# Layer 3 of a four-layer graph network: projections copied in pairs from two PSUM banks, and the first two aggregations of a group issued ahead of the next projection

## The chip, the core and the metric

The kernel runs on one core of one Trainium2 chip. The metric is the device time of one execution in microseconds (us). The core has five engines that work side by side, each through its own list of instructions in order: TensorE (PE, matrix products), VectorE (DVE), ScalarE (ACT), GpSimd (POOL) and SyncE (SP, which here only issues transfers). They meet through semaphores: an instruction waits until a counter has reached a value. PSUM, into which TensorE writes its products, has eight banks of 128 x 512 f32.

## The reference, cut to what matters

64 graphs of 128 nodes with 256 features each pass through four layers. After each layer comes a residual sum and a layer norm. The last layer, which the change touches, is per graph:

```python
def _L3_gnn_ref(x, A_shape, w, a):
    y = x @ w
    s = y @ a
    A = s[..., :, None] + s[..., None, :]
    A = jnp.tanh(A / 8.0) * 8.0
    A = jnp.where(A >= 0, A, 0.1 * A)
    A = jnp.exp(A) * A_shape
    A = A / jnp.sum(A, axis=-1, keepdims=True)
    A = A * jnp.sum(A_shape, axis=-1, keepdims=True)
    return A @ x @ w
x = _layernorm(x + _L3_gnn_ref(x, adj, w, a))
```

## The kernel before, in words

The graphs are worked on in 16 groups (g) of four graphs (j = 0 to 3). Each layer is a software pipeline: every engine has a function `step(g, p, has)` that issues its work for one step, for groups at different stages. `has(0)` is the group g itself, `has(-1)` the one before. No planner sets the order: it is written out by hand in these functions, and each engine keeps to it. Only at the seams between two layers do the steps of both layers alternate, by strings such as `SEAMS_PE`.

In layer 3 the work of a group is this.

1. TensorE makes the node scores from the transposed features xT (`node_scores`, 24 products of one column, lines 87 to 89). VectorE splits them in two halves (`split_scores`, lines 1502 and 1504).
2. TensorE spreads the scores over a 128 x 512 tile (`spread_scores`, line 1514, 8 products). ScalarE takes the tanh in four operations (line 1982), VectorE the leaky step (line 2028), ScalarE the exponential (line 1989). GpSimd multiplies by the adjacency and gives U (line 2076, `attention`).
3. TensorE makes x @ w of each graph (`project(g, p, j)`, 6 products of 256 columns at lines 87 to 89), graphs 0 and 2 in one bank, graphs 1 and 3 in the next (`b_xw[j % 2]`). ScalarE copies each to SBUF (`copy_xw`, line 1974), and only then may its bank be written again.
4. TensorE multiplies U by that copy in f32 (`aggregate(g, p, j)`, line 1947, two records for a graph). VectorE scales by the row factors and adds the residual (lines 2035 to 2045), takes the statistics (line 1085), GpSimd forms the scales (lines 1104 to 1113), and ScalarE applies the norm (`norm_apply`, line 1119).
5. For later groups ScalarE and GpSimd split x into f16 halves (`x_high`, line 1164, and `x_low`, line 1171), and SyncE has them transposed by DMA into xT (line 1185), two steps ahead.

TensorE's step before is: projections 2 and 3 of group g-1; node scores of g; projection 0 of g; spread of g; aggregation 0 of g-1; projection 1 of g; aggregations 1, 2 and 3 of g-1.

ScalarE's step before is: copies 0 and 1 of g; exponential of g; `x_high` of g+2; copy 2 of g; norm 0 and 1 of g-2; copy 3 of g; norm 2 of g-2; the four tanh of g+1; norm 3 of g-2.

GpSimd's step is `x_low`, the norm scales, then U of g+1. VectorE's is: row factors and residuals of g-2, scores of g, statistics and variance of g-2, leaky step of g.

The semaphore `xw_ps` counts projections, `xw_ok` counts copies, `out_ps` counts aggregations, `u_ok` counts U.

Of the kernel before, what the change touches and what calls it, by code (L numbers as in the profile page):

```python
# [8 lines left out]
ACT = mybir.ActivationFunctionType  # L9
AX = mybir.AxisListType  # L10

GRAPHS, N, D, H = 64, 128, 256, 512
GP = 4
# [26 lines left out]
def upto(g, per, k):  # L40

    return g * per + k
# [17 lines left out]
def is_first(g):  # L60
    return isinstance(g, int) and g == 0
# [18 lines left out]
def reused(g, back=2):  # L80

    return not isinstance(g, int) or g >= back


def triple(nc, out, lhs, rhs, start=True, stop=True, **kw):

    nc.tensor.matmul(out, lhs[0], rhs[1], start=start, stop=False, **kw)  # L87
    nc.tensor.matmul(out, lhs[1], rhs[0], start=False, stop=False, **kw)  # L88
    return nc.tensor.matmul(out, lhs[0], rhs[0], start=False, stop=stop, **kw)  # L89
# [963 lines left out]
def norm(nc, ctx, tag, deep=2, tiles=None):  # L1053

    L = Parts()
    L.deep = deep
    tiles = tiles or ctx

    def sb(name, shape):
        made = [tiles.enter_context(nc.sbuf_tensor(f"{tag}_{name}{i}", shape, F32)) for i in range(deep)]  # L1060
        return [made[p % deep] for p in range(2)]

    L.pre, L.st = sb("pre", [128, GP, D]), sb("st", [128, GP, 6])
    L.veps, L.rstd, L.nmr = (sb(name, [128, GP]) for name in ("veps", "rstd", "nmr"))
    L.mdiff, L.m2, L.dd, L.msum, L.mneg = (tiles.enter_context(nc.sbuf_tensor(f"{tag}_{name}", [128, GP], F32))
                                           for name in ("mdiff", "m2", "dd", "msum", "mneg"))
    L.pre_ok, L.st_ok, L.agg, L.mean_ok, L.rstd_ok, L.nmr_ok, L.x_new = (
        ctx.enter_context(nc.semaphore(f"{tag}_{name}"))
        for name in ("pre_ok", "st_ok", "agg", "mean_ok", "rstd_ok", "nmr_ok", "x_new"))
    return L  # L1070
# [103 lines left out]
def transposed(F, eng, g, p):  # L1174

    eng.wait_ge(F.xT_in[p], 16 * (F.base + g - p) + 32)
# [287 lines left out]
def attention_front(nc, K, ctx, layer, width):  # L1464

    S = Parts()
    S.s_ps, S.s_hi, S.s_lo, S.s_bias, S.sj_ps, S.t_ok, S.e_ok, S.u_ok = (
        ctx.enter_context(nc.semaphore(f"l{layer}_{name}"))
        for name in ("s_ps", "s_hi", "s_lo", "s_bias", "sj_ps", "t_ok", "e_ok", "u_ok"))
    S.s = [ctx.enter_context(nc.sbuf_tensor(f"l{layer}_s_{s}", [128, GP], F16)) for s in ("hi", "lo")]  # L1470
    S.bias = ctx.enter_context(nc.sbuf_tensor(f"l{layer}_bias", [128, GP], F32))
    S.t = ctx.enter_context(nc.sbuf_tensor(f"l{layer}_t", [128, C], F32))
    if layer == 3:
        S.lr = ctx.enter_context(nc.sbuf_tensor(f"l{layer}_lr", [128, C], F32))
    S.e = ctx.enter_context(nc.sbuf_tensor(f"l{layer}_e", [128, C], F32))
    S.u = ctx.enter_context(nc.sbuf_tensor(f"l{layer}_u", [128, C], F32))
    S.width, S.layer = width, layer
    return S


def node_scores(nc, K, F, S, pe, g, p, b, weights, column):

    if is_first(g):
        for done, count in K.scores_after[S.layer]:
            pe.wait_ge(done, count)
    transposed(F, pe, g, p)
    if reused(g, 1):
        pe.wait_ge(S.s_lo, upto(g - 1, 1, 1))
        pe.wait_ge(S.s_bias, upto(g - 1, 1, 1))
    for j in range(GP):  # L1490
        for d in range(DT):
            m = triple(nc, b[:, j * S.width:(j + 1) * S.width], [s[:, j, d, :] for s in F.xT[p]],
                       [w[:, d, column:column + S.width] for w in weights], start=d == 0, stop=d == DT - 1)
    m.then_inc(S.s_ps, 1)
# [393 lines left out]
def layer3(nc, K, ctx):  # L1888

    def sb(name, shape, dt=F32):  # L1890
        return ctx.enter_context(nc.sbuf_tensor(f"l3_{name}", shape, dt))

    def sem(name):
        return ctx.enter_context(nc.semaphore(f"l3_{name}"))

    bank = K.bank[2:4] + K.bank[0:2] + K.bank[4:8]
    b_s, b_t, b_xw, b_out = bank[0], bank[1], bank[2:4], bank[4:8]
    sums = K.banks[:, 4 * 512:8 * 512].rearrange("p (g c) -> p g c", g=GP)[:, :, D]
    L, S = norm(nc, ctx, "l3"), attention_front(nc, K, ctx, 3, 1)
    us = [sb(f"U{p}", [128, C]) for p in range(2)]  # L1900

    xw = [sb(f"xw{p}", [128, GP, D + 1]) for p in range(2)]
    rrec, rfac = sb("rrec", [128, GP]), [sb(f"rfac{p}", [128, GP]) for p in range(2)]
    lr_ok, xw_ps, xw_ok, xw_one, out_ps, rrec_ok, rfac_ok = map(
        sem, ("lr_ok", "xw_ps", "xw_ok", "xw_one", "out_ps", "rrec_ok", "rfac_ok"))
# [21 lines left out]
    def tensor(pe):  # L1927
        def project(g, p, j):
            if j < 2 and is_first(g):
                pe.wait_ge(K.far_lo, upto(G - 1, GP, 3 + j))  # L1930
            if j >= 2 or reused(g, 1):
                pe.wait_ge(xw_ok, upto(g, GP, j - 1))
            for d in range(DT):
                m = triple(nc, b_xw[j % 2][:, 0:D], [s[:, j, d, :] for s in F.xT[p]],
                           [w[:, d, 0:D] for w in K.w3], start=d == 0, stop=d == DT - 1)
            m.then_inc(xw_ps, 1)

        def aggregate(g, p, j):
            if j == 0:
                pe.wait_ge(S.u_ok, upto(g, 1, 1))  # L1940
            if is_first(g):
                pe.wait_ge(xw_one, 2)
                pe.wait_ge(K.hr_ok, upto(G - 1, GP, j + 1))
            pe.wait_ge(xw_ok, upto(g, GP, j + 1))
            if reused(g, 1):
                pe.wait_ge(L.pre_ok, upto(g - 1, GP, j + 1))
            pe.matmul(b_out[j][:, 0:D + 1], us[p][:, j * N:(j + 1) * N], xw[p][:, j, :], start=True,
                      stop=True).then_inc(out_ps, 1)

        def step(g, p, has):  # L1950
            q = 1 - p
            if has(-1):
                project(g - 1, q, 2)
                project(g - 1, q, 3)
            if has(0):
                node_scores(nc, K, F, S, pe, g, p, b_s, K.w3, D)
                project(g, p, 0)
                spread_scores(nc, K, S, pe, g, b_t, S.t_ok, GP)
            if has(-1):
                aggregate(g - 1, q, 0)  # L1960
            if has(0):
                project(g, p, 1)
            if has(-1):
                aggregate(g - 1, q, 1)
                aggregate(g - 1, q, 2)
                aggregate(g - 1, q, 3)
        return step, 0, 1

    def scalar(act):
        def copy_xw(g, p, j):  # L1970
            act.wait_ge(xw_ps, upto(g, GP, j + 1))
            if reused(g):
                act.wait_ge(out_ps, upto(g - 2, GP, j + 1))
            act.activation(xw[p][:, j, 0:D], b_xw[j % 2][:, 0:D], ACT.Copy).then_inc(xw_ok, 1)

        def tanh(g, j):
            if j == 0:
                act.wait_ge(S.sj_ps, upto(g, 1, 1))
                act.wait_ge(S.s_bias, upto(g, 1, 1))
                if reused(g, 1):  # L1980
                    act.wait_ge(lr_ok, upto(g - 1, 1, 1))
            act.activation(S.t[:, j * N:(j + 1) * N], b_t[:, j * N:(j + 1) * N], ACT.Tanh,
                           bias=S.bias[:, j:j + 1], scale=0.125).then_inc(S.t_ok, 1)

        def exponentials(g):
            act.wait_ge(lr_ok, upto(g, 1, 1))
            if reused(g, 1):
                act.wait_ge(S.u_ok, upto(g - 1, 1, 1))
            act.activation(S.e[:], S.lr[:], ACT.Exp, scale=8.0).then_inc(S.e_ok, 1)

        def step(g, p, has):
            q = 1 - p
            if has(0):
                copy_xw(g, p, 0)
                copy_xw(g, p, 1)
                exponentials(g)
            if halves_due(F, g + 2):
                x_high(K, F, L, act, g + 2, p)
            if has(0):
                copy_xw(g, p, 2)  # L2000
            if has(-2):
                norm_apply(K, L, act, g - 2, p, 0)
                norm_apply(K, L, act, g - 2, p, 1)
            if has(0):
                copy_xw(g, p, 3)
            if has(-2):
                norm_apply(K, L, act, g - 2, p, 2)
            if has(1):
                tanh(g + 1, 0)
                tanh(g + 1, 1)  # L2010
                tanh(g + 1, 2)
                tanh(g + 1, 3)
            if has(-2):
                norm_apply(K, L, act, g - 2, p, 3)
        return step, 2, 2

    def vector(dve):
# [92 lines left out]
```

## Time and profile before

| what | value |
|---|---|
| median of 3 runs | 669.33 us (668.38 to 669.84) |
| profiled execution, its own time | 670.21 us |
| its span, first to last instruction | 668.1 us |
| PE busy | 622.3 us, 93% of the span |
| DVE busy | 564.5 us, 84% |
| ACT busy | 524.2 us, 78% |
| POOL busy | 380.5 us, 57% |

Busy time is the sum of the spans of an engine's instructions. Matmuls overlap in the pipeline, so a busy PE is not a PE at its peak. An idle stretch is put down to the instruction whose semaphore released it. The profiled execution took 2.1 us more than its span, which lies around the first and the last instruction.

### The profile page before, as it was taken

How to read it: one execution, taken by the hardware profiler on the slowest of the kernel's cores; microseconds unless marked ns; L12 is line 12 of the kernel's file. 1: busy time of each engine (PE TensorE's matmuls, PEld its weight loads, DVE VectorE, ACT ScalarE, POOL GpSimd, SP SyncE). 2: the span in 40 equal slices, each digit the busy share in tenths (PEclk: the TensorE clock that was granted, in tenths of full speed). 3: DMA queues.
4: the chain of work that ended last, by engine and by line, in shares of the span. 5: the costliest groups of instructions: out<-in, count | busy, mean ns of one | idle time of the engine just before them, and what ended most of it. 6: DMA issues, size and time to landing. Idle time of an engine off the chain costs nothing.

```text
span 668.1 us, 15720 instructions
## 1 busy us (share of the span) xinstructions
PE 622.3 (93%) x4950; PEld 449.4 (67%) x4950; DVE 564.5 (84%) x1696; ACT 524.2 (78%) x1183; POOL 380.5 (57%) x448
## 2 busy tenths in 40 slices
PE   5989999999999998999999989999999997999993
PEld 4667777777777775566666656666666664787882
DVE  3799998888998988778898898899889887688886
ACT  4557888878777777768999788787878775899995
POOL 1144556676665657756777444344434343899983
PEclk9999999999999999998999999999999998999998
DMA  9592337464757436344655334554544542488883
GB/s 272 177 229 57 80 65 204 96 160 95 164 104 174 100 78 81 64 94 85 103 100 96 64 80 95 96 95 97 96 96 93 98 88 57 82 189 186 185 184 126
DMA packets 176769, 78.24 MB, mean 117 GB/s; under 512 B 123440, under 2 KB 175152, under 8 KB 176688
## 3 DMA queue, kind: packets, MB, share of 16 engines
q1 hardware_dynamic: 166512, 68.46, 45.4%
q0 software_dynamic: 8448, 8.39, 8.7%
q8 instruction: 40, 0.66, 0.4%
q10 hardware_dynamic: 1728, 0.40, 0.3%
q14 instruction: 41, 0.34, 0.2%
HBM read 31.07 MB, written 8.40 MB: 59 GB/s over the span
## 4 chain that ended last, share of the span: by engine, by line
PE 26%; POOL 9%; DVE 8%; DMA 8%; ACT 2%; issue 2%; SPq 0%; POOLq 0%; ACTq 0%; DVEq 0%
PE banks L87 8%; PE banks L89 7%; PE banks L88 7%; DMA xT_lo<-x_halves 6%; POOL x_halves L1171 4%; DVE l_st L1085 3%; POOL l_rstd L1110 2%; POOL l_U L2076 2%; PE banks L1265 1%; DMA l_TT_lo<-l_T_lo 1%; PE banks L1633 1%; PE banks L1277 1%; DVE l_pre L1367 1%; POOL l_T_lo L1873 1%; ACT x_resident L1119 0%
## 5 line engine op out<-in xcount | busy, mean ns | idle before, releaser
L1119 ACT ACTIVATE x_resident<-l_pre,l_nmr,l_rstd 128x256 f32<-128x256 f32 x256 | 140.6, 601 | 7.7 <-POOL l_nmr L1113 7.7
L1011 POOL TENSOR_TENSOR hq<-hq 128x512 f32<-128x512 f32 x48 | 75.1, 1565 | 86.8 <-ACT hq L706 84.5
L1171 POOL TENSOR_TENSOR x_halves<-x_resident,x_halves 128x1024 f16<-128x1024 f32 x46 | 98.2, 2134 | 16.5 <-DVE l_pre L1367 9.9
L1085 DVE BATCH_NORM_STATS2 l_st<-l_pre 128x6 f32<-128x256 f32 x256 | 93.4, 411 | 0.0
L87 PE MATMUL banks<-Wk_lo,xT_hi 128*128 128x512 f16 (+1 forms) x256 | 83.5, 326 | 5.6 <-DMA xT_lo<-x_halves 2.5
L88 PE MATMUL banks<-Wk_hi,xT_lo 128*128 128x512 f16 (+1 forms) x256 | 83.3, 325 | 0.0
L89 PE MATMUL banks<-Wk_hi,xT_hi 128*128 128x512 f16 (+1 forms) x256 | 83.2, 325 | 0.0
L1110 POOL TENSOR_TENSOR l_rstd<-l_veps,minus_half 128x4 f32<-128x4 f32 x64 | 71.8, 1122 | 19.2 <-DVE l_veps L1099 16.2
L87 PE MATMUL banks<-W2T_lo,h_hi 128*128 128x257 f16 x256 | 70.2, 274 | 2.4 <-DVE h_lo L869 1.3
L89 PE MATMUL banks<-W2T_hi,h_hi 128*128 128x257 f16 x256 | 70.1, 274 | 0.0
L88 PE MATMUL banks<-W2T_hi,h_lo 128*128 128x257 f16 x256 | 70.1, 274 | 0.0
L693 ACT ACTIVATE hf<-banks,b_col 128x512 f32<-128x512 f32 x64 | 44.2, 691 | 26.2 <-PE banks L89 25.9
L87 PE MATMUL banks<-xT_lo,W1T_hi 128*128 128x512 f16 x128 | 48.7, 381 | 2.3 <-DVE xT_lo L889 1.1
L1873 POOL TENSOR_TENSOR l_T_lo<-l_tf,l_T_hi 128x512 f16<-128x512 f32 x16 | 18.5, 1157 | 55.2 <-ACT l_T_hi L1724 55.2
L869 DVE TENSOR_TENSOR h_lo<-hf,h_hi 128x512 f16<-128x512 f32 x64 | 42.7, 699 | 8.0 <-issue 5.6
L1164 ACT ACTIVATE x_halves<-x_resident 128x1024 f16<-128x1024 f32 x46 | 48.6, 1056 | 0.1
L87 PE MATMUL banks<-w_lo,xT_hi 128*128 128x1 f16 (+1 forms) x256 | 45.3, 221 | 3.5 <-DMA xT_lo<-x_halves 2.4
L89 PE MATMUL banks<-xT_hi,W1T_hi 128*128 128x512 f16 x128 | 48.5, 379 | 0.0
L88 PE MATMUL banks<-xT_hi,W1T_lo 128*128 128x512 f16 x128 | 48.5, 379 | 0.0
L1104 POOL TENSOR_TENSOR l_msum<-l_st 128x4 f32<-128x4 f32 x64 | 13.4, 210 | 59.1 <-DVE l_st L1085 58.4
L88 PE MATMUL banks<-w_hi,xT_lo 128*128 128x1 f16 (+1 forms) x256 | 46.2, 220 | 0.0
L89 PE MATMUL banks<-w_hi,xT_hi 128*128 128x1 f16 (+1 forms) x256 | 46.0, 220 | 0.0
(201 smaller groups left out, 1923.5 us busy)
## 6 DMA issues: line engine op xcount, KB each, us to landing
adj<-in_adj SPq DMA_DIRECT2D x32, 256.0 KB, 4.1
x_halves<-in_x SPq DMA_DIRECT2D x16, 512.0 KB, 4.3
x_resident<-b_half SPq DMA_DIRECT2D x8, 1024.0 KB, 7.8
x_resident<-in_x POOLq DMA_DIRECT2D x16, 512.0 KB, 6.1
out<-x_resident SPq DMA_DIRECT2D x15, 512.0 KB, 3.2
dbc<-degree_rows SPq DMA_DIRECT2D x8, 256.0 KB, 3.8
x_resident<-in_L_gnn_W SPq DMA_DIRECT2D x2, 512.0 KB, 5.4
x_resident<-in_L_gnn_Wk SPq DMA_DIRECT2D x1, 768.0 KB, 9.6
```

Of the source, the lines that this page charges most:

```text
L87: nc.tensor.matmul(out, lhs[0], rhs[1], start=start, stop=False, **kw)
L88: nc.tensor.matmul(out, lhs[1], rhs[0], start=False, stop=False, **kw)
L89: return nc.tensor.matmul(out, lhs[0], rhs[0], start=False, stop=stop, **kw)
L693: act.activation(hf[:, h, :], b_hid[h % 2][:], ACT.Relu, bias=K.b1[:, h:h + 1], scale=1.0 / W_SCALE).then_inc(hf_ok, 1)
L869: dve.tensor_tensor(hs[1][:, h, :], hf[:, h, :], hs[0][:, h, :], ALU.subtract).then_inc(h_lo, 1)
L1011: pool.tensor_tensor(hq[:, 0, :], hq[:, 0, :], hq[:, h, :], ALU.add).then_inc(hqs_ok, 1)
L1085: dve.bn_stats(L.st[p][:, j, :], L.pre[p][:, j, :]).then_inc(L.st_ok, 1)
L1110: pool.tensor_tensor(L.rstd[p][:], L.veps[p][:], K.minus_half[:], ALU.pow).then_inc(L.rstd_ok, 1)
L1119: act.activation(K.x[:, gcols(g, j)], L.pre[p][:, j, :], ACT.Identity, bias=L.nmr[p][:, j:j + 1], scale=L.rstd[p][:, j:j + 1]).then_inc(L. ...
L1164: act.activation(F.xs[p][0], x_group(K, g), ACT.Copy).then_inc(F.x_hi, 1)
L1171: pool.tensor_tensor(F.xs[p][1], x_group(K, g), F.xs[p][0], ALU.subtract).then_inc(F.x_lo, 1)
L1873: pool.tensor_tensor(ts[1][:], tf[:], ts[0][:], ALU.subtract).then_inc(t_lo, 1)
```

## The change

ScalarE copies the projections of two graphs by one operation, which reads 256 columns of each of the two banks (`pair_xw`, 128 x 2 x 256, f32). So 64 copies of 128 x 256 become 32 of 128 x 512. The semaphore `xw_ok` counts pairs. Each copy waits for both projections of its pair, and a projection waits until the pair that was in both banks has been copied. Copy 3, which stood behind norm 1, is now part of the second pair's copy, ahead of norm 0. On TensorE, aggregations 0 and 1 of group g-1 now stand between the node scores of g and projection 0 of g.

```diff
+    pair_xw = K.banks[:, 0:2 * 512].rearrange("p (j c) -> p j c", j=2)[:, :, 0:D]
...
         def project(g, p, j):
             if j < 2 and is_first(g):
                 pe.wait_ge(K.far_lo, upto(G - 1, GP, 3 + j))
             if j >= 2 or reused(g, 1):
-                pe.wait_ge(xw_ok, upto(g, GP, j - 1))
+                pe.wait_ge(xw_ok, upto(g, 2, j // 2))
...
         def aggregate(g, p, j):
-            pe.wait_ge(xw_ok, upto(g, GP, j + 1))
+            pe.wait_ge(xw_ok, upto(g, 2, j // 2 + 1))
...
                 project(g - 1, q, 3)
             if has(0):
                 node_scores(nc, K, F, S, pe, g, p, b_s, K.w3, D)
+            if has(-1):
+                aggregate(g - 1, q, 0)
+                aggregate(g - 1, q, 1)
+            if has(0):
                 project(g, p, 0)
                 spread_scores(nc, K, S, pe, g, b_t, S.t_ok, GP)
-            if has(-1):
-                aggregate(g - 1, q, 0)
-            if has(0):
                 project(g, p, 1)
             if has(-1):
-                aggregate(g - 1, q, 1)
                 aggregate(g - 1, q, 2)
                 aggregate(g - 1, q, 3)
...
-        def copy_xw(g, p, j):
-            act.wait_ge(xw_ps, upto(g, GP, j + 1))
+        def copy_pair(g, p, k):
+            act.wait_ge(xw_ps, upto(g, GP, 2 * k + 2))
             if reused(g):
-                act.wait_ge(out_ps, upto(g - 2, GP, j + 1))
-            act.activation(xw[p][:, j, 0:D], b_xw[j % 2][:, 0:D], ACT.Copy).then_inc(xw_ok, 1)
+                act.wait_ge(out_ps, upto(g - 2, GP, 2 * k + 2))
+            act.activation(xw[p][:, 2 * k:2 * k + 2, 0:D], pair_xw, ACT.Copy).then_inc(xw_ok, 1)
...
             if has(0):
-                copy_xw(g, p, 0)
-                copy_xw(g, p, 1)
+                copy_pair(g, p, 0)
                 exponentials(g)
             if halves_due(F, g + 2):
                 x_high(K, F, L, act, g + 2, p)
             if has(0):
-                copy_xw(g, p, 2)
+                copy_pair(g, p, 1)
             if has(-2):
                 norm_apply(K, L, act, g - 2, p, 0)
                 norm_apply(K, L, act, g - 2, p, 1)
-            if has(0):
-                copy_xw(g, p, 3)
             if has(-2):
                 norm_apply(K, L, act, g - 2, p, 2)
```

## Rows read from the trace of the kernel before

**Rows 1.** Busy time by stage: us, each engine, PE clock granted, DMA.

```profile
582.42:652.02 69.60, 67.33 (x769) 56.26 (x769) 58.35 (x217) 66.49 (x167) 62.89 (x72) 1.00 0.84 181
560.00:570.00 10.00, 7.38 (x93) 5.79 (x91) 5.14 (x23) 4.82 (x13) 3.15 (x6) 0.83 0.21 41
```

**Rows 2.** Waits in 582.4 to 652 us: total us, times, longest.

```profile
PE banks L87 <- DMA xT_lo<-x_halves: 2.2, 7, 0.7
ACT l_t L1982 <- PE banks L1514: 2.0, 6, 0.6
```

**Rows 3.** Chain that ended last, 592 to 606 us: start, duration, what.

```profile
598.40 2.10 POOL x_halves L1171
600.52 3.28 DMA xT_lo<-x_halves
603.85 0.18 PE banks L87
```

**Rows 4.** Timeline of ACT, one step: start, us, instruction, [idle before].

```profile
605.77 1.14 ACT L1982 ACTIVATE l_t<-banks,l_bias 128x128 f32<-128x128 f32 x4 [0.36 <-PE banks L1514]
...
607.28 0.67 ACT L1974 ACTIVATE l_xw<-banks 128x256 f32<-128x256 f32 x2
607.80 0.66 ACT L1989 ACTIVATE l_e<-l_lr 128x512 f32<-128x512 f32 x1
608.32 1.09 ACT L1164 ACTIVATE x_halves<-x_resident 128x1024 f16<-128x1024 f32 x1
```

**Rows 5.** Timeline of PE, the same step.

```profile
605.12 0.22 PE L1514 MATMUL banks<-ident,l_s_lo 128*128 128x128 f16 x1
...
605.57 0.65 PE L1947 MATMUL banks<-l_xw,l_U 128*128 128x257 f32 x2
606.06 0.27 PE L87 MATMUL banks<-w_lo,xT_hi 128*128 128x256 f16 x1
...
606.72 1.47 PE L1947 MATMUL banks<-l_xw,l_U 128*128 128x257 f32 x6
...
608.02 0.27 PE L87 MATMUL banks<-w_lo,xT_hi 128*128 128x256 f16 x1
...
609.34 0.17 PE L87 MATMUL banks<-w_lo,xT_hi 128*128 128x1 f16 x1
```

**Rows 6.** Timeline of ACT: tanh of groups 1, 2, 3 and 15, what follows.

```profile
569.82 1.14 ACT L1982 ACTIVATE l_t<-banks,l_bias 128x128 f32<-128x128 f32 x4 [1.10 <-PE banks L1514]
570.83 2.07 ACT L1119 ACTIVATE x_resident<-l_pre,l_nmr,l_rstd 128x256 f32<-128x256 f32 x4
572.80 0.65 ACT L1974 ACTIVATE l_xw<-banks 128x256 f32<-128x256 f32 x2
...
576.82 1.14 ACT L1982 ACTIVATE l_t<-banks,l_bias 128x128 f32<-128x128 f32 x4 [1.36 <-PE banks L1514]
...
578.72 0.63 ACT L1989 ACTIVATE l_e<-l_lr 128x512 f32<-128x512 f32 x1 [0.21 <-DVE l_lr L2028]
...
582.42 1.14 ACT L1982 ACTIVATE l_t<-banks,l_bias 128x128 f32<-128x128 f32 x4
...
652.02 1.14 ACT L1982 ACTIVATE l_t<-banks,l_bias 128x128 f32<-128x128 f32 x4 [0.63 <-PE banks L1514]
```

**Rows 7.** Timeline of PE where layer 3 begins.

```profile
564.45 0.42 PE L87 MATMUL banks<-w_lo,xT_hi 128*128 128x256 f16 x1
...
569.74 0.70 PE L1947 MATMUL banks<-l_xw,l_U 128*128 128x257 f32 x2
...
573.23 0.28 PE L87 MATMUL banks<-w_lo,xT_hi 128*128 128x256 f16 x1 [0.83 <-ACT l_xw L1974]
```

**Rows 8.** ACT instructions that read PSUM, by line: duration ns min/median/max, stretch, form.

```profile
L743 ACT ACTIVATE adjT_resident<-banks x16: 594/614/643, 5.5 to 244.2; 128x512 f32<-128x512 f32 x16
```

**Rows 9.** Timelines of POOL and PE, the last U and aggregations.

```profile
655.04 1.27 POOL L2076 TENSOR_TENSOR l_U<-l_e,adjT_resident 128x512 f32<-128x512 f32 x1
...
656.37 2.01 PE L1947 MATMUL banks<-l_xw,l_U 128*128 128x257 f32 x8 [0.62 <-POOL l_U L2076]
```

## The prediction, made before the change was run

> **What bounds the kernel now.** I read the page first: layer 3 is only the last sixth of the span, so the change can act between about 565 us and the end. The second view is busy time by stage. In the 69.60 us from the tanh of group 3 to that of group 15, PE is busy 67.33 us, ACT 66.49, POOL 62.89, DVE 58.35, at a granted clock of 1.00 [rows 1]. Those are 12 steps, so a step takes 69.60 / 12 = 5.80 us, and no engine has more than a tenth free. The third view, the waits, shows how little slack there is between them: PE waits 2.2 us in all for the transposed features, ACT 2.0 us in all for the spread of the scores [rows 2]. The fourth, the chain that ended last, names what is late by those microseconds: GpSimd's low half of x (2.10 us), its transposing DMA (3.28 us), then node scores [rows 3]. So a step is near PE's and ACT's own work, with a transfer just behind. In such a pipeline the question is not how much work an edit takes away but which ring of dependences it closes from one step to the next.
>
> **The change, part by part.** *The pair copy as work of ACT.* Two copies of 128x256 now take from 607.28 to 607.80 before ACT goes on, 0.52 us. A 128x512 exponential holds ACT from 607.80 to 608.32, again 0.52 us [rows 4]. The new copy has as many elements as the two old ones, so I put the gain in ACT's own time at zero, within 0 and 0.05 us a pair (between the two lies only the fixed part of one start, which these equal pitches don't show).
>
> The Trainium skill (Perfetto Trace Analysis, Optimizing Scalar/DVE Operations) gives an access overhead of about 51 ns for each ScalarE operation on PSUM and says that larger operations help a saturated engine. By that page 32 operations fewer are an estimate of 1.6 us if ACT were the bound; the pitches above show nothing of it. It is the base of the second rival below.
>
> *The pair copy as a wait.* Before, projection 2 waited only for copy 0, and projection 0 of the next group only for copy 2: two banks in turn. Now both banks are held until a pair is copied, and then both are free at once. What is queued behind the waiting projection 2 on PE: projection 3, node scores, aggregations 0 and 1, projection 0, the spread; ACT's next tanh waits for that spread. How long the pair copy takes no row shows for two banks. From below: one 128x256 copy, 0.41 us or less. From above: the two in a row, 0.67 us [rows 4]. The nearest row is a 128x512 read of one bank, 0.614 us [rows 8]; I take 0.61.
>
> *The moved aggregations.* Aggregation 0 took 605.57 to 606.06, 0.49 us, and three in a row 606.72 to 608.02, 1.30 us [rows 5], so two in a row cost 0.49 + 0.43 = 0.92 us, and PE's sum for a step stays. But they now stand ahead of projection 0 and the spread, so the tanh comes later by 0.92 us after the node scores, and they put the wait for U ahead of the spread too. Before, both hung behind the spread, where ACT didn't need them.
>
> **The ring that this closes.** From one tanh to the next:
> - four tanh and norm 3 to the start of the copies, 605.77 to 607.28: 1.51 us [rows 4];
> - the pair copy 0.61 us;
> - its end to PE's start: 0.06 us. Of two copies that took 0.65 from 572.80 on, 0.26 to 0.28 apart, the first ended at 573.17 to 573.19; PE began at 573.23 [rows 6, 7];
> - projections 2 and 3, 608.02 to 609.34: 1.32 us [rows 5];
> - node scores and projection 0: 603.85 to 605.12, 1.27 us [rows 3, 5];
> - aggregations 0 and 1, in between: 0.92 us;
> - spread to tanh, 605.12 to 605.77: 0.65 us [rows 4, 5].
>
> Sum: 6.34 us a step. Each link is either the order of one engine or a semaphore, so no overlap shortens it. Without the aggregations and with the first 256-column copy alone (0.39 us) the same ring was 5.20 us, and did not bind.
>
> A second ring, through U: the exponential starts 2.03 us after the tanh (605.77 to 607.80) and takes 0.66 [rows 4]; to GpSimd I take 0.07, like the step from ACT to PE; U takes 1.27 and PE starts 0.06 after it (655.04 to 656.31, 656.37) [rows 9]; then 0.92, projection 0 (606.06 to 606.72, 0.66 us) and 0.65. Sum: 6.32 us. So even a pair copy that cost nothing extra would leave a step at 6.32. Both give +0.54 or +0.52 us on 5.80.
>
> The transfer is then not what is late: U ends 4.03 us after the tanh, the low half 2.10 later, the DMA 3.28 later, 0.05 to PE: 9.46. The node scores that need it are due at 3.50 + 6.34 = 9.84. It has 0.38 us to spare; a longer DMA by 0.6 us would cost 0.1 us a step.
>
> **The start.** Group 1: U of group 0 still lets PE go at 569.74 [rows 7]; then two aggregations (0.53 and 0.43 there), 0.66, 0.65: tanh at 572.01 instead of 569.82, +2.19. Group 2: four norms of layer 2 stand between tanh and copy, 569.82 to 572.80 = 2.98 [rows 6], so 2.98 + 0.61 + 0.06 + 1.32 + 1.27 + 0.92 + 0.65 = 7.81: tanh at 579.82 instead of 576.82, +3.00. Group 3: no norm there, and the ring through U decides: exponential 1.90 after the tanh (576.82 to 578.72), 0.63 + 0.07 + 1.27 + 0.06 + 0.92 + 0.66 + 0.65 = 6.16: 585.98 instead of 582.42, +3.56. From group 3 to 15: 12 x 0.54 = +6.5.
>
> **The end.** U of group 15 starts 3.02 us after its tanh now (652.02 to 655.04), held by GpSimd's norm scales; with slower steps those are done before, and it starts at 2.03 + 0.66 + 0.07 = 2.76: -0.26. What follows the last aggregations is unchanged.
>
> Sum: 3.56 + 6.5 - 0.26 = +9.8 us. On the profiled execution's own time: 670.21 + 9.8 = 680.0. Its median stands 0.88 us lower: 669.33 + 9.8 = 679.1 us.
>
> **The rivals.**
>
> 1. *Only the start is paid.* The moved aggregations (0.92 us) lie just where PE would wait for the second pair (0.61 + 0.06), and hide it. If the first pair were hidden too, steps stay at 5.80: 3.56 - 0.26 = +3.3, 672.6 us. For it: PE's work in a step is the same. Against: the ring of 6.34 has no link that can be left out. It decides only if the tanh did not wait for the spread, and the waits show that it does, six times even now. Chance 0.08.
>
> 2. *Faster: ACT is the bound and has less to do.* ACT is without work for 3.1 of 69.60 us [rows 1]. If the step followed ACT, 0.05 us a pair over 32 pairs gives -1.6 us; with the start covered by its present waits (1.10 and 1.36 us ahead of the tanh, [rows 6]) 667.7 us. It decides from where the ring is shorter than 5.80, that is if copy, aggregations and node scores ran 0.54 us faster than their rows. Chance 0.04.
>
> 3. *The clock falls.* PE's own work in a step is about (69.60 - 2.2) / 12 = 5.6 us [rows 1, 2], so it now idles 6.34 - 5.6 = 0.7 us, in one wait at projection 2 or in two. In 560 to 570 us, after PE had waited over 2 us, the granted clock was 0.83 in the mean, so part of it at the lower level of 1.2 GHz, and a 256-column product took 0.42 instead of 0.27 us [rows 1, 7]. At half rate the products of the ring other than node scores (1.32 + 0.92 + 0.66 + 0.45) add about 3.3 us to a step; three such steps give 689 us. Against: a wait of 0.83 us at 573.23 left the clock at 1.00 right after. Chance 0.06. The Trainium skill (TensorE: Matmul & The Clock Gate, A second HAM failure mode: psum-queue depth-cycling) tells of such a kernel, whose small idle times between matmul groups made the clock swing; the rows here have no case of it.
>
> **How the numbers follow.** The forecast has 0.80. Its own range is 677 to 682: the pair copy between 0.41 (the ring through U holds 6.32) and 0.67 (+0.06 over 14 steps, +0.8), and 0.1 us a step either way for changes between f32 and f16 products and for the DMA (1.4 us), and 1 us for the start. The range for 8 in 10 is widened towards the first rival and to a few slow steps: 675 to 684. About 0.2% (1.3 us) is what a measurement of this kernel can tell from no change. Faster by more than that: 0.04 (rival 2). Within: 0.02, for cases with no name here. Slower: 0.94 (forecast, rivals 1 and 3).
>
> **What would show it.** Tanh starts about 6.3 us apart from group 3 on; PE idle about 0.7 us a step, ahead of projection 2 for the pair copy or ahead of aggregation 0 for U; ACT idle ahead of the tanh; PE waits no more for the transposed features; a pair copy of 0.6 us; clock at 1.00. The prediction is wrong if the pitch stays near 5.8, or if PE's wait is for something not in either ring.

## The result

| | before | changed |
|---|---|---|
| median of the comparison | 668.86 us (4 runs, 665.80 to 669.84) | 678.51 us (4 runs, 675.29 to 680.13) |
| profiled execution, its own time | 670.21 us | 677.19 us |
| span | 668.1 us | 675.4 us |
| tanh of group 0 to the end of the span | 103.40 us | 115.22 us |
| step, tanh of group 3 to that of group 15 | 5.80 us | 6.363 us |

The ratio is 1.0159, with a 95% interval of 1.0125 to 1.0192: slower, by 9.65 us between the medians. The forecast was 679.1 us, +9.8, in a range of 675 to 684.

The two profiles differ by more in layer 3 (11.8 us) than in the span (7.3 us), because the first tanh of layer 3 stands at 560.18 us in the changed kernel and at 564.70 in the kernel before, though no instruction ahead of it was changed. The section on the prediction comes back to this ("The first tanh"); layer 3 is therefore compared from its own first tanh.

### The profile page after: what moved, and what is told of

It is laid out like the page before. It is cut to its first block, busy times and chain, and to the rows that moved or that the text cites. A ratio compares the mean times of both kernels' runs of the same rounds, so it can differ in the third digit from the quotient of the medians.

```text
span 675.4 us, 15660 instructions
## 1 busy us (share of the span) xinstructions
PE 621.4 (92%) x4950; PEld 448.1 (66%) x4950; DVE 564.2 (84%) x1696; ACT 524.4 (78%) x1151; POOL 378.9 (56%) x448
## 4 chain that ended last, share of the span: by engine, by line
PE 35%; ACT 6%; DVE 5%; DMA 4%; POOL 3%; issue 3%; SPq 0%; ACTq 0%; POOLq 0%; DVEq 0%
PE banks L87 10%; PE banks L89 9%; PE banks L88 9%; DMA xT_lo<-x_halves 3%; PE banks L1948 2%; ACT x_resident L1119 2%; ACT l_t L1983 2%; DVE l_st L1085 1%; PE banks L1265 1%; POOL x_halves L1171 1%; PE banks L1514 1%; ACT l_xw L1975 1%; POOL l_rstd L1110 1%; DMA l_TT_lo<-l_T_lo 1%; PE banks L1633 1%
## 5 line engine op out<-in xcount | busy, mean ns | idle before, releaser
L1119 ACT ACTIVATE x_resident<-l_pre,l_nmr,l_rstd 128x256 f32<-128x256 f32 x256 | 138.1, 595 | 6.9 <-POOL l_nmr L1113 6.8
L1171 POOL TENSOR_TENSOR x_halves<-x_resident,x_halves 128x1024 f16<-128x1024 f32 x46 | 98.2, 2135 | 15.7 <-DVE l_pre L1367 9.1
L1110 POOL TENSOR_TENSOR l_rstd<-l_veps,minus_half 128x4 f32<-128x4 f32 x64 | 65.9, 1029 | 20.1 <-DVE l_veps L1099 16.7
L87 PE MATMUL banks<-w_lo,xT_hi 128*128 128x1 f16 (+1 forms) x256 | 47.2, 223 | 11.9 <-ACT l_xw L1975 11.9
```

The source lines that it names most:

```text
L1110: pool.tensor_tensor(L.rstd[p][:], L.veps[p][:], K.minus_half[:], ALU.pow).then_inc(L.rstd_ok, 1)
L1119: act.activation(K.x[:, gcols(g, j)], L.pre[p][:, j, :], ACT.Identity, bias=L.nmr[p][:, j:j + 1], scale=L.rstd[p][:, j:j + 1]).then_inc(L. ...
L1171: pool.tensor_tensor(F.xs[p][1], x_group(K, g), F.xs[p][0], ALU.subtract).then_inc(F.x_lo, 1)
```

## The profile after

Busy time by stage, from the tanh of group 3 to that of group 15 (us; PE, PE's weight loads, DVE, ACT, POOL, then the PE clock, DMA share, GB/s) answers to [rows 1]:

```profile
583.24:659.60 76.36, 68.16 (x770) 57.03 (x769) 58.02 (x216) 66.80 (x144) 60.68 (x71) 1.00 0.73 163
```

76.36 / 12 = 6.363 us a step. Every engine has nearly the work it had (ACT 66.80 after 66.49, PE 68.16 after 67.33), with 23 ACT instructions fewer. Only the stretch is longer: no engine is slower, they wait. The 23 starts saved gave ACT nothing.

The waits in 583 to 660 us (us in total, times, longest) answer to [rows 2]:

```profile
PEld banks L87 <- ACT l_xw L1975: 13.0, 12, 1.1
DVE l_lr L2026 <- ACT l_t L1983: 11.1, 12, 1.0
POOL l_U L2074 <- ACT l_e L1990: 9.4, 12, 0.8
PE banks L87 <- ACT l_xw L1975: 8.2, 12, 0.7
ACT l_t L1983 <- PE banks L1514: 8.0, 13, 0.8
```

The wait for the transposed features is gone. In its place PE waits for the pair copy once a step (8.2 us over 12 steps), ACT's tanh for PE's spread, VectorE for the tanh, GpSimd for the exponential. Each link of a ring waits for the one before it: that is how a ring looks in this view.

The chain that ended last, of one step (start, duration, what), answers to [rows 3]:

```profile
627.30 0.46 PE banks L1514 x8
627.81 0.24 issue
628.05 0.41 ACT l_t L1983 x2
628.55 0.38 ACT l_t L1983
628.93 0.48 ACT x_resident L1119
629.41 0.50 ACT l_xw L1975
629.96 0.28 PE banks L87
...
632.03 0.98 PE banks L1948 x4
...
633.66 0.46 PE banks L1514 x8
```

DMA and GpSimd have left the chain. From spread to spread it is 6.36 us: spread, tanh, norm 3, pair copy, projections, aggregations, projection, spread.

ACT's timeline of the same step (start, us, instruction, [idle before]) answers to [rows 4]:

```profile
627.78 1.14 ACT L1983 ACTIVATE l_t<-banks,l_bias 128x128 f32<-128x128 f32 x4 [0.60 <-PE banks L1514]
628.80 0.61 ACT L1119 ACTIVATE x_resident<-l_pre,l_nmr,l_rstd 128x256 f32<-128x256 f32 x1
629.29 0.61 ACT L1975 ACTIVATE l_xw<-banks 128x512 f32<-128x512 f32 x1
629.77 0.65 ACT L1990 ACTIVATE l_e<-l_lr 128x512 f32<-128x512 f32 x1
...
634.15 1.14 ACT L1983 ACTIVATE l_t<-banks,l_bias 128x128 f32<-128x128 f32 x4 [0.60 <-PE banks L1514]
```

And PE's answers to [rows 5]:

```profile
628.24 1.03 PE L1948 MATMUL banks<-l_xw,l_U 128*128 128x257 f32 x4
629.96 0.28 PE L87 MATMUL banks<-w_lo,xT_hi 128*128 128x256 f16 x1 [0.68 <-ACT l_xw L1975]
...
631.28 0.17 PE L87 MATMUL banks<-w_lo,xT_hi 128*128 128x1 f16 x1
...
631.89 1.12 PE L1948 MATMUL banks<-l_xw,l_U 128*128 128x257 f32 x4
632.84 0.27 PE L87 MATMUL banks<-w_lo,xT_hi 128*128 128x256 f16 x1
...
633.50 0.22 PE L1514 MATMUL banks<-ident,l_s_lo 128*128 128x128 f16 x1
```

The links of the forecast can be read off one by one: tanh to copy 1.51 us (1.51 forecast), copy 0.61 (0.61), copy end 629.90 to PE 0.06 (0.06), projections 2 and 3 1.32 (1.32), node scores and projection 0 0.61 + 0.66 (1.27), two aggregations 0.95 (0.92), spread to tanh 0.65 (0.65). Only the aggregations were off, by 0.03. The second ring stood just behind: U, which GpSimd began at 630.49 and worked on for 1.28 us, was ready at 631.77, 0.12 us before PE began the aggregations, where the forecast allows 0.06 from U to PE.

## The experiments

Theory A is that of the prediction: what stands between one tanh and the next closes a ring, and the two aggregations ahead of the spread put two rings over 5.80 us. Theory B is that the lost double buffering of the two banks costs the time by itself. Two more theories come with the expectations: C has one ring only, that of the pair copy, and D has it that one of the two aggregations is free. The steps below are each run's, from the tanh of group 3 to that of group 15, out of the row of busy time by stage; layer 3 is from the first tanh to the end of the span. Step and layer 3 come from one profiled execution, the median from all; they need not fit each other to the microsecond.

| run | step, us | layer 3, us | median, us | ratio to before (95%) |
|---|---|---|---|---|
| before | 5.80, again 5.76 | 103.4, 103.5 | | |
| changed | 6.363, again 6.360 | 115.2, 115.4 | 678.51 | 1.0159 (1.0125 to 1.0192) |
| pair copies only | 5.745 | 105.4 | 671.24 | 1.0042 (1.0013 to 1.0072) |
| moved aggregations only | 6.379 | 113.7 | 678.76 | 1.0159 (1.0111 to 1.0207) |
| spread between aggregations | 5.798 | 106.2 | 668.23 | 1.0014 (0.9979 to 1.0048) |
| norm 3 late | 6.438 | 115.1 | 680.57 | 1.0181 (1.0119 to 1.0243) |
| one aggregation ahead | 5.932 | 107.1 | 673.78 | 1.0086 (1.0051 to 1.0122) |
| norm 3 between | 6.317 | 114.5 | one run, 678.66 | |
| early copy | 6.363 | 113.4 | one run, 674.46 | |
| statistics ahead | 5.837 | 104.7 | 667.69 | 1.0015 (0.9987 to 1.0043) |

**Pair copies only.** The changed kernel with TensorE's order of before:

```diff
-            if has(-1):
-                aggregate(g - 1, q, 0)
-                aggregate(g - 1, q, 1)
             if has(0):
                 project(g, p, 0)
                 spread_scores(nc, K, S, pe, g, b_t, S.t_ok, GP)
+            if has(-1):
+                aggregate(g - 1, q, 0)
+            if has(0):
                 project(g, p, 1)
             if has(-1):
+                aggregate(g - 1, q, 1)
                 aggregate(g - 1, q, 2)
```

> Pair copies as in the change, TensorE's order as before (aggregation 0 behind the spread, 1 to 3 behind projection 1). Theory A (two rings close only when aggregations 0 and 1 stand ahead of the spread): the ring is 1.51 + 0.61 + 0.06 + 1.32, then projection 0 waits for the second pair, 0.16 + 0.61 + 0.06 = 0.83 instead of node scores' 0.62, then 0.66 + 0.65 = 5.6 us, under the 5.80 of before. Step 5.8 us, PE waits 0.2 us a step ahead of projection 0, 669 to 671 us. Theory B (the lost double buffering alone costs it, the aggregations only fill the wait): step 6.3 us or more, 677 us or more, since nothing covers the second copy now.

Busy time by stage, and PE's weight loads' wait for the copy in 585 to 655 us:

```profile
579.72:648.66 68.94, 67.94 (x769) 56.63 (x769) 58.85 (x218) 65.72 (x143) 62.40 (x71) 1.00 0.81 181
```
```profile
PEld banks L87 <- ACT l_xw L1975: 1.9, 12, 0.2
```

68.94 / 12 = 5.745 us. The wait for the second pair is there, 0.2 us a step as expected, and costs nothing in the step, which is now PE's own work of 5.66 us and little else (weight loads also waited 4.0 us in 11 waits for the transposed features; PE's matmuls show no such wait). Theory B is out for the steps. The median of 671.24 is 0.2 us over what was expected. What the pair copies cost in this profile lies at the start: the three intervals up to the tanh of group 3 are 6.68 + 7.12 + 6.58 = 20.4 us, against 17.7 before (18.3 in the second profile of before). PE waited 1.22 us for a copy there, against 0.83 before [rows 7]; what makes up the rest was not taken apart. Layer 3 is 2.0 us longer and the median 3.4, so 1.5 us of the median is not placed.

**Moved aggregations only.** The kernel before, with PE's order of the changed one and single copies:

```diff
+            if has(-1):
+                aggregate(g - 1, q, 0)
+                aggregate(g - 1, q, 1)
+            if has(0):
                 project(g, p, 0)
                 spread_scores(nc, K, S, pe, g, b_t, S.t_ok, GP)
-            if has(-1):
-                aggregate(g - 1, q, 0)
-            if has(0):
                 project(g, p, 1)
             if has(-1):
-                aggregate(g - 1, q, 1)
                 aggregate(g - 1, q, 2)
```

> Single copies as before, aggregations 0 and 1 of the group before ahead of projection 0 as in the change. Theory A: the ring through U stands whole, 6.3 us, though the ring through the copies is only 1.51 + 0.39 + 0.06 + 1.32 + 1.27 + 0.92 + 0.65 = 6.12. Step 6.3 us, 677 to 679 us; PE's wait moves from projection 2 to aggregation 0, released by U. Theory B: step near 5.8, 669 to 670 us.

```profile
584.65:661.20 76.55, 70.11 (x770) 57.76 (x769) 60.27 (x218) 66.88 (x168) 60.90 (x72) 1.00 0.71 163
```

76.55 / 12 = 6.379 us, and the same ratio as the change, 1.0159. So the moved aggregations alone account for it. The expectation on the wait half missed: PE's matmuls still waited for a copy (5.1 us in 11 waits), and only weight loads waited for U, 1.6 us in 10 waits. But the longer wait is not the one that holds the step. One step of this run (start, us, instruction, [idle before]; ACT's tanh ahead of it started at 597.41):

```profile
599.37 0.28 PE L87 MATMUL banks<-w_lo,xT_hi 128*128 128x256 f16 x1 [0.46 <-ACT l_xw L1974]
...
600.18 1.28 POOL L2076 TENSOR_TENSOR l_U<-l_e,adjT_resident 128x512 f32<-128x512 f32 x1 [0.85 <-ACT l_e L1989]
...
601.51 0.73 PEld L1947 LDWEIGHTS banks<-l_xw,l_U 128*128 128x128 f32 x4 [0.16 <-POOL l_U L2076]
601.51 1.14 PE L1947 MATMUL banks<-l_xw,l_U 128*128 128x257 f32 x4
...
603.79 1.14 ACT L1982 ACTIVATE l_t<-banks,l_bias 128x128 f32<-128x128 f32 x4 [0.74 <-PE banks L1514]
```

Projection 2 waits 0.46 us for the first copy. Projections 2 and 3 and the node scores (1.32 + 0.61) are then done at 601.30, and PE stands until U is ready at 601.46. From there on it goes 0.05 to PE and 2.28 to the next tanh, 6.38 us in all from tanh to tanh. Through the copies alone it would have been 0.21 less, 6.17 (an estimate from these rows; 6.12 was expected). So with single copies the ring through U holds the step, as theory A had it.

**Spread between.** The changed kernel with another order on PE:

```diff
             if has(-1):
                 aggregate(g - 1, q, 0)
-                aggregate(g - 1, q, 1)
             if has(0):
-                project(g, p, 0)
                 spread_scores(nc, K, S, pe, g, b_t, S.t_ok, GP)
+            if has(-1):
+                aggregate(g - 1, q, 1)
+            if has(0):
+                project(g, p, 0)
                 project(g, p, 1)
```

> Pair copies; TensorE: node scores, aggregation 0, spread, aggregation 1, projections 0 and 1, aggregations 2 and 3. Theory A: one aggregation and no projection ahead of the spread; ring 1.51 + 0.61 + 0.06 + 1.32 + 0.62 + 0.49 + 0.65 = 5.26, through U 2.03 + 0.66 + 0.07 + 1.27 + 0.06 + 0.49 + 0.65 = 5.2; the pair copies stay covered. Step between PE's own 5.6 and the transfer's 5.8 us, 666 to 670 us. Theory B (pairs cost by themselves): 674 us or more.

```profile
583.80:653.37 69.57, 69.21 (x770) 55.05 (x770) 58.40 (x218) 66.58 (x144) 59.98 (x72) 1.00 0.81 180
```

5.798 us, and 668.23 us, no difference from the kernel before that can be told. Both aggregations are still ahead of projection 0, and the pairs are still there; only the spread is earlier. What costs is not where the aggregations stand toward the projection, as the change is worded, but what stands ahead of the spread: this edit takes aggregation 1 (0.43) and projection 0 (0.66) out of both rings at once, and does not part the two. The next run moves one aggregation alone. Layer 3 of this profile is 2.8 us longer than before, all of it in the first three intervals (7.70 + 6.82 + 6.09 = 20.6 us): PE's granted clock was 0.50 up to about 570 us there, so how much of it is the order and how much the clock stays open.

**One aggregation ahead.** Aggregation 0 stays ahead of projection 0, aggregation 1 goes back:

```diff
                 aggregate(g - 1, q, 0)
-                aggregate(g - 1, q, 1)
...
             if has(-1):
+                aggregate(g - 1, q, 1)
                 aggregate(g - 1, q, 2)
```

> The changed kernel with only aggregation 0 ahead of projection 0; aggregation 1 goes back behind projection 1. Theory A (what stands ahead of the spread adds one for one to both rings): the step falls by one aggregation, 0.43, from 6.36 to 5.93 us, still over 5.80; time 671 to 672.5 us. Theory D (a step is either on the ring or not; one aggregation is free): step 5.75, 669 to 670 us.

```profile
579.09:650.27 71.18, 68.19 (x770) 56.97 (x769) 59.14 (x217) 66.81 (x144) 57.75 (x72) 1.00 0.77 175
```

71.18 / 12 = 5.932 us, the 5.93 of theory A: one for one. The median of 673.78 is 1.3 us over the range; layer 3 is 3.7 us longer than before and the medians differ by 6.7. The profiled execution took 668.65 us, the shortest of eight, so the other 3.0 us is not in this profile.

**Norm 3 late, and norm 3 between.** Two tries to shorten the copy's ring alone. The first:

```diff
                 copy_pair(g, p, 0)
                 exponentials(g)
+            if has(-3):
+                norm_apply(K, L, act, g - 3, q, 3)
```

> The changed kernel with ScalarE's norm 3 (of the group two back) moved behind the first pair's copy and the exponential of the next step, so that it is no longer between the tanh and the copy. Theory A (both rings near each other): the copy's ring falls by 0.50 to 5.86, the ring through U only by 0.1 to 0.15, since the exponential then waits for VectorE's leaky step (1.90 us after the tanh): step 6.15 to 6.2 us, 675 to 677 us, PE's wait now ahead of aggregation 0. Theory C (the pair copy's ring alone binds): step 5.9 us, 672 to 673 us.

It came out at 6.438 us, longer than with norm 3 in its place, and the median 3.6 us over the range, which neither theory had. The waits in 585 to 655 us:

```profile
DVE l_pre L2045 <- ACT x_resident L1119: 10.8, 11, 1.0
PE banks L87 <- DMA xT_lo<-x_halves: 3.1, 5, 1.1
```

VectorE's residual writes a buffer that norm 3 reads, waited 0.98 us for it in every step, and carried the delay to the scores, the statistics, GpSimd and the transfer, whose ring of two steps was back. The second has norm 3 between the copy and the exponential, so that neither is late:

```diff
                 copy_pair(g, p, 0)
+            if has(-3):
+                norm_apply(K, L, act, g - 3, q, 3)
+            if has(0):
                 exponentials(g)
```

> The changed kernel with ScalarE's norm 3 between the first pair's copy and the exponential, so that the copy starts 1.01 instead of 1.51 us after the tanh, while the exponential and VectorE's residual (which needs norm 3) stay in time. Theory A: the copy's ring falls to 5.86, the ring through U stays; step 6.29 to 6.32 us, PE's wait ahead of aggregation 0, released by U. Theory C (only the copy's ring binds, and the wait of VectorE hid it in the run with norm 3 still later): step 5.9 us.

```profile
585.25:661.05 75.80, 70.44 (x770) 57.51 (x769) 60.69 (x217) 65.45 (x143) 61.02 (x73) 1.00 0.76 164
```
```profile
PE banks L1948 <- POOL l_U L2077: 2.2, 8, 0.3
```

75.80 / 12 = 6.317 us, with PE now waiting for U ahead of aggregation 0 (its wait for the copy is down to 2.1 us in 11 waits). The copy's ring was shortened by 0.5 us and the step by 0.046: the second ring is real, at the 6.32 that the prediction had. Theory C, one ring, is out. ACT is 65.45 us busy of 75.80 here; it is not the bound.

**Early copy.** At the start of layer 3, group 1's first pair copy and exponential ahead of layer 2's last norms:

```diff
-            if has(0):
+            if has(0) and g != 1:
                 copy_pair(g, p, 0)
                 exponentials(g)
...
                 tanh(g + 1, 3)
+            if g == 0:
+                copy_pair(1, 1, 0)
+                exponentials(1)
```

> The changed kernel with group 1's first pair copy and exponential ahead of layer 2's last four norms on ScalarE instead of behind them. PE's wait of 2.14 us at projection 2 of group 1, after which the clock fell for some products, falls to about 0.7 us. Then the tanh of group 2 is held by VectorE instead, whose residual waits for those norms: 4.5 us after the tanh, then 1.6 for four residuals, 0.35 for the scores' halves, 0.65 for the spread: 7.1 us from the tanh of group 1 to that of group 2 (7.83 at full clock, 9.22 in the profile of the changed kernel). Steps of 6.36 us after that; total 0.5 us less at most than the changed kernel's usual time. If the clock had not fallen because of that wait, the products of that stretch show the lower rate here too.

PE in 562 to 580 us:

```profile
568.23 0.28 PE L87 MATMUL banks<-w_lo,xT_hi 128*128 128x256 f16 x1 [0.20 <-ACT l_xw L1975]
...
571.70 1.11 PE L1948 MATMUL banks<-l_xw,l_U 128*128 128x257 f32 x4 [1.40 <-DVE l_pre L2046]
```

The interval was 7.41 us, not 7.1: PE's wait at the projection fell to 0.20 us, and a new one of 1.40 came at aggregation 0, whose bank VectorE's residual had not yet read, as the residual waits for those norms. The aggregation, once moved ahead, meets that wait too; I had looked only at the spread. The products behind it ran at the upper rate (four aggregation records in 1.11 us). That alone doesn't show that the longer wait brings the clock down, since it stayed up behind such a wait in another run (below). The steps are 6.363 us, as in the changed kernel.

**Statistics ahead.** The kernel before, with VectorE's first row of statistics ahead of the next scores:

```diff
                 residual(g - 2, p, 3)
+                norm_row(L, dve, g - 2, p, 0)
             if has(0):
                 scores(g)
```

> The kernel before, with VectorE's first row of statistics (0.33 us) ahead of the scores of the next group. Theory A (the step before is held by the transfer's ring of two steps, 11.8 us, only where node scores are late): every late step gets shorter by up to 0.33 us, step 5.65 to 5.75 instead of 5.80, 0.6 to 1.8 us less. Rival: the split scores come 0.33 us later and the spread waits for them, step 5.8 to 5.9.

```profile
583.64:653.68 70.04, 68.15 (x769) 56.19 (x769) 58.01 (x217) 66.98 (x167) 58.23 (x72) 1.00 0.82 179
```

5.837 us: the rival, 5.8 to 5.9. In 585 to 655 us the spread's weight loads waited 4.1 us for the low half of the scores. No version tried beats the kernel before.

**Both kernels again.**

> The changed kernel once more, nothing altered. If the fall of the clock after PE's wait of 2.14 us at projection 2 of group 1 belongs to that execution and not to the change, the tanh of group 2 comes 7.8 or 9.2 us after that of group 1, and all else is as in the first profile: steps of 6.36 us, 15.8 us from the last tanh to the end. The layers ahead of the change were 4.5 us shorter in the first profile than in that of the kernel before; if that is spread between executions, they may lie anywhere from 559 to 565 us here.

> The kernel before once more, nothing altered: steps of 5.80 us from group 3 to 15 and about 103.4 us from the first tanh to the end of the span; that first tanh anywhere from 559 to 565 us if the start of layer 3 is a matter of the execution, at 564.7 if it belongs to the kernel.

Changed: steps of 6.360 us, 115.4 us of layer 3, 15.7 us after the last tanh, first tanh at 559.96. Before: steps of 5.762, 103.5 us, first tanh at 563.42. The first two intervals of the changed kernel were 9.28 and 7.82 us here, and 7.61 and 9.22 in the first profile. Here PE's granted clock was 0.50 in the whole of 563 to 571 us, from the seam on; PE's wait at projection 2 of group 1 was 1.18 us, and the clock stayed at 1.00 behind it. The runs with norm 3 late (7.32, 7.83) and with the aggregations alone (7.31, 7.83) had both short.

## Why the prediction was right

- *ACT gains nothing from larger copies.* Shown: copy to exponential 0.48 us, for two copies 0.52 [rows 4], and ACT's busy time is the same. The gain was 0.04 us a pair, at the upper end of 0 to 0.05, and lay off the ring that binds (it is in the one through U: exponential 1.99 us after the tanh, 2.03 before). The Trainium skill (Perfetto Trace Analysis, Optimizing Scalar/DVE Operations) gives about 51 ns of access overhead for a ScalarE operation on PSUM; the 0.04 us saved with each operation is near it. Its condition for a gain, a saturated engine, did not hold. Rival 2 is out.
- *The step.* 6.34 forecast, 6.363 measured. Links, order and both rings were as said: the first binds in the changed kernel (6.36), and the second, through U, wherever the first is shorter: at 6.32 with norm 3 between, at 6.38 with single copies.
- *One reading was wrong.* "No engine has more than a tenth free" does not hold for VectorE: its 58.35 of 69.60 us [rows 1] leave 16% free. Nothing in the sum rests on it.
- *Which edit.* The prediction summed the copy's ring with both edits in it, and said that a pair copy at no cost would still leave 6.32 us. The runs part the edits: the aggregations alone make 1.0159, as much as both together, and the pair copies alone 1.0042, of which the profile shows only what lies at the start.
- *The start.* Forecast 7.31, 7.81 and 6.16 us for the first three intervals. They were 7.31, 7.83 and 6.25 in the run with the moved aggregations only, where the granted clock was 0.56 in 563 to 566 us and 1.00 in 566 to 582. In both profiles of the changed kernel one interval was longer by 1.4 to 2.0 us. There the products ran at the lower rate. In the second interval of the first profile the same four aggregation records took 2.06 us, against 1.12 in the profile of the changed kernel again:

```profile
571.42 0.28 PE L87 MATMUL banks<-w_lo,xT_hi 128*128 128x256 f16 x1 [2.14 <-ACT l_xw L1975]
...
573.58 2.06 PE L1948 MATMUL banks<-l_xw,l_U 128*128 128x257 f32 x4
```

So rival 3 came true in a small part: not in the steady steps, where PE waits 0.68 us and the granted clock is 1.00, but once at the start. In the first profile that was behind a wait of 2.14 us, in the second ahead of it, where the lower rate from the seam lasted longer. The prediction's links imply the wait (PE is done with its aggregations at about 569.3 and the pair is copied at 571.4), but it is not written down there, and the clock has no price at the start.
- *The end.* 15.80 us from the last tanh, 15.82 forecast.
- *The sum.* 7.61 + 9.22 + 6.23 + 76.36 + 15.80 = 115.2 us, against 113.2 forecast from the first tanh: 2.0 us over, 1.7 of it in the first two intervals and 0.3 in the steps. With the moved aggregations only, where no interval was long, it was 113.7.
- *Luck in the total.* The forecast, +9.8 us, is a sum over layer 3 alone, and layer 3 grew by 11.8 us between the two profiles. That the medians differ by 9.65, within 0.2 us of the forecast, is in part luck: the profiles have 2.0 us more in layer 3 and the medians 2.2 us less outside it. How many of the executions without a profile had a long interval at the start is not on record.
- *The first tanh.* It stood at 558.9 to 563.2 us in the eight profiles of kernels with pair copies, and at 563.3 to 565.0 in the four with single copies, with the same instructions ahead of it. The granted clock around 300 us sorts the twelve in another way. In five, the rows of 300 to 310 us have a clock of 1.00, and the first tanh stands at 558.9 to 560.2; in the other seven the clock is 0.69 to 0.83, and it stands at 562.3 to 565.0. Here are the changed kernel, the kernel before, and the spread between aggregations, which has pair copies too:

```profile
300.00:310.00 10.00, 10.00 (x68) 6.71 (x69) 9.46 (x35) 8.13 (x20) 7.80 (x10) 1.00 0.49 94
300.00:310.00 10.00, 8.12 (x44) 4.95 (x43) 7.75 (x26) 7.04 (x17) 7.68 (x10) 0.83 0.39 67
300.00:310.00 10.00, 8.12 (x44) 4.77 (x42) 7.62 (x26) 6.97 (x18) 7.47 (x9) 0.83 0.42 70
```

Three of the eight kernels with pair copies are among the seven, so the pair copies don't decide it. Part of the distance is older than this fall: layer 1's copies (line 1322) began at 284.5 us in the kernel before and at 282.3 in the changed one. The medians show no effect of the pair copies either: if these started layer 3 some 3 us earlier, medians would differ from before by 3 us less than layer 3 does. They differ by 2.2 us less (changed), 1.5 more (pair copies only), 2.4 less (spread between), 1.1 more (norm 3 late) and 3.0 more (one aggregation ahead), which has no common sign.

**Open.** Why the clock falls at about 300 us in some executions and not in others, why layer 1 begins up to 4 us apart, and how often either happens: no run was made for it.

## What to carry to other kernels

In a pipeline whose busiest engines have almost nothing free (here PE and ScalarE, 97% and 96%), add up each ring from one step's instruction to the same one in the next, in issue order, before moving anything: an instruction is free behind the one that another engine waits for, and costs its full time ahead of it. Here 0.95 us of matmuls, unchanged in number, made a step 0.56 us longer; issuing the spread (0.45 us) between them, and so ahead of projection 0 too, brought the step back to 5.80 us. Merging two copies from two banks saves almost nothing where starts overlap anyway, and holds both banks until both have been copied; here the kernel with pair copies alone was 2.7 us longer in its first three intervals and nowhere else in the layer, though it is not shown that the held banks are the whole reason.

## What the runs showed of the hardware

- A ScalarE copy of 2 x 256 f32 columns from two adjacent banks takes 0.58 to 0.62 us, 0.60 in the median of 32, as much as 512 columns of one bank (0.614, [rows 8]).
- After the same wait of PE of 2.14 us, at the same place in the program, the next products ran at the upper rate in one profile (four aggregation records in 1.11 us, norm 3 late) and at the lower in two (2.06 us, changed and norm 3 between). One wait of that length decides nothing by itself.
- Where layer 3 begins, the granted clock was 0.50 in every profile, and it was back at 1.00 by 566 us in the changed kernel and not before 571 us in the same kernel run again. The two executions took 677.19 and 678.75 us.
